# Summing two weight matrices in wider ScalarE passes, a first weight load in two halves, and new instruction sequences, in a fused attention and feed-forward kernel

## What is computed

```python
# attention part, per batch
Q, K = h @ Wq.T, h @ Wk.T                       # h: context, 4 heads
sim = einsum('bhnd,bhmd->bnm', Q, K) / (sqrt(d) * H)
threshold = top_k(sim, 153)[0][:, :, -1:]       # the 153rd largest of each row of 512
A = sigmoid(sim) * (sim >= threshold)
A = (A + A.T) * 0.5
x = x + (1 - gamma) * layernorm(x) + gamma * A
# feed-forward part
def weight_quant(w): s = 1 / clip(mean(abs(w)), 1e-5); return round(clip(w * s, -1, 1)) / s
def bitlinear(x, w): return act_quant(rmsnorm(x)) @ weight_quant(w).T
y = layernorm(x)
x = x + bitlinear(silu(bitlinear(y, w_gate)) * bitlinear(y, w_up), w_down)
```

## Time and profile before

| | |
|---|---|
| runs | 271.83, 271.90, 272.65 us; median 271.9 |
| profiled execution, own time | 272.7 us |
| its span in the trace | 269.8 us |
| busy: PE, DVE | 215.5 us (80%), 215.6 us (80%) |
| busy: ACT, POOL | 192.0 us (71%), 171.2 us (63%) |
| PE weight loads (beside the matmuls) | 105.0 us |
| DMA | 39.18 MB, mean 145 GB/s |
| mean granted PE clock | 0.911 |

### The profile page before, as it was taken

The page is one execution under the profiler, slowest core; times in us unless marked ns, Lnnn a source line. Parts: engine busy times, 40 slices in busy tenths (PEclk is TensorE's granted clock), DMA queues, the critical chain, the costliest instruction groups (busy, mean ns, idle before and its releaser), DMA issues.

```text
span 269.8 us, 3680 instructions
## 1 busy us (share of the span) xinstructions
PE 215.5 (80%) x947; PEld 105.0 (39%) x958; DVE 215.6 (80%) x379; ACT 192.0 (71%) x325; POOL 171.2 (63%) x324
## 2 busy tenths in 40 slices
PE   7744501503986896799999999999999999999985
PEld 7212101402733352343445444444544444444432
DVE  0368987998879998997999899897988787488381
ACT  2488995999999999998988967663619185241420
POOL 2045798885886868788977778886661823408330
PEclk9965755565799999999999999999999999999999
DMA  4999999979849478364104044306096115190675
GB/s 129 392 348 386 388 327 188 420 187 214 151 81 161 78 88 157 69 117 90 31 1 79 2 78 88 88 0 101 10 244 140 39 36 140 19 197 12 125 201 206
DMA packets 78998, 39.18 MB, mean 145 GB/s; under 512 B 67968, under 2 KB 70272, under 8 KB 78464
## 3 DMA queue, kind: packets, MB, share of 16 engines
q1 hardware_dynamic: 78976, 38.94, 58.6%
...
## 4 chain that ended last, share of the span: by engine, by line
PE 31%; ACT 20%; issue 15%; DVE 15%; POOLq 6%; POOL 6%; DMA 4%; DVEq 3%; ACTq 0%
PE U L394 10%; PE DN L413 10%; PE G L380 9%; ACT junk_c L491 6%; ACT S L540 5%; DVE S L741 4%; DMA S<-S 3%; ACT WdT L533 3%; DVE amh L746 2%; DVE m L607 2%; ACT sg L516 2%; ACT junk_x L505 1%; PE TR L413 1%; POOLq L911 1%; POOL X L935 1%
## 5 line engine op out<-in xcount | busy, mean ns | idle before, releaser
L380 PE MATMUL G<-WgT,xqT 128*128 128x512 bf16 x256 | 60.5, 379 | 4.7 <-ACT sg L516 4.6
L516 ACT ACTIVATE sg<-G,gsc 128x1024 f32<-128x1024 f32 x32 | 35.6, 1112 | 40.2 <-PE G L380 36.1
L394 PE MATMUL U<-WuT,xqT 128*128 128x512 bf16 x256 | 60.5, 379 | 1.7 <-DVE S L741 1.2
L491 ACT ACTIVATE junk_c<-rows,srch 128x512 int8<-128x512 f32 (+1 forms) x72 | 51.1, 716 | 5.0 <-POOL srch L904 3.3
L741 DVE TENSOR_TENSOR S<-U,sg 128x1024 f32<-128x1024 f32 x32 | 39.0, 1218 | 14.2 <-PE U L394 11.6
L1000 POOL TENSOR_SCALAR S<-S,qh 128x2048 int16<-128x2048 f32 x15 | 31.1, 2076 | 24.7 <-DVE qh L790 23.0
L413 PE MATMUL DN<-WdT,S 128*128 128x512 bf16 x198 | 45.7, 379 | 0.5
L380 PEld LDWEIGHTS G<-WgT,xqT 128*128 128x128 bf16 x256 | 24.5, 98 | 36.4 <-issue 5.5
L394 PEld LDWEIGHTS U<-WuT,xqT 128*128 128x128 bf16 x256 | 24.5, 98 | 33.7 <-DVE S L741 5.0
L746 DVE TENSOR_REDUCE amh<-S 128x1 f32<-128x2048 f32 x15 | 34.0, 2270 | 0.1
L524 ACT ACTIVATE junk_h<-S 128x2048 int8<-128x2048 f32 x16 | 30.5, 1903 | 3.7 <-DVE S L741 3.6
...
## 6 DMA issues: line engine op xcount, KB each, us to landing
...
S<-S SPq DMA_TRANSPOSE x17, 4.3
```

Of the source, the lines that this page charges most:

```text
L380: last = nc.tensor.matmul(G[:, c * 512:(c + 1) * 512], xqT[:, t, k, :], WgT[:, 4 * n:4 * n + 4, k, :], start=(k == 0), stop=(k == KD - 1))
L394: last = nc.tensor.matmul(U[:, c * 512:(c + 1) * 512], xqT[:, t, k, :], WuT[:, 4 * n:4 * n + 4, k, :], start=(k == 0), stop=(k == KD - 1))
L491: A(junk_c[:, j, :].bitcast(U8) if r == ROUNDS else junk_c[:, j, :], ROWS[a % 2][:, j, :], ACT.Sign, bias=nthr[:, j:j + 1], accum_out=cs[: ...
L516: A(sg[:, u % 2, :], G[:, :], ACT.Silu, scale=gsc[:, b % 2, t:t + 1]).then_inc(silu_done, 1)
```

## The change

Three edits:

1. Up's and down's weight sums on ACT are made in two passes of 4096 columns (`w_abs2`), not four of 2048. A pass waits for both its groups and counts as two. Their sums are added over 2 columns, not 4. (`w_round2` is defined and not called.)
2. Gate's group 0 is loaded by two DMAs of 0.5 MB, each with its own semaphore, and DVE sums it in two halves of 1024 columns (`w_abs_half`). Gate's sums are added over 5 columns.
3. All five lists are made anew.

```diff
-        wsum = sb("wsum", [P, 3, 4])
+        wsum = sb("wsum", [P, 3, 5])
...
+        s_wh = [sem(f"s_wh{h}") for h in range(2)]
...
-        n_dve = [4 * (w + 1) - n_act[w] for w in range(3)]
+        n_dve = [4 * (w + 1) + 1 - n_act[w] for w in range(3)]
+        N_SUMS = (5, 2, 2)
...
+            def w_load_half(w, h):
+
+                sp.dma_start(STAGE[w][:, h * GROUP // 2:(h + 1) * GROUP // 2].rearrange("p (c d) -> p c d", d=D),
+                             w_gate[h * 256:(h + 1) * 256, :].rearrange("(c p) d -> p c d", p=P)).then_inc(s_wh[h], 16)
...
-                nc.tensor.matmul(DN[:, 0:4], onesf[:, :], wsum[:, w, :], start=True, stop=True).then_inc(s_wtot, 1)
+                nc.tensor.matmul(DN[:, 0:N_SUMS[w]], onesf[:, :], wsum[:, w, 0:N_SUMS[w]], start=True,
+                                 stop=True).then_inc(s_wtot, 1)
...
+            def w_abs2(w, g):
+
+                for k in (g, g + 1):
+                    act.wait_ge(s_win[w][k], 16)
+                act.wait_ge(s_wabs_act, n_act[w - 1])
+                if w == 2:
+                    act.wait_ge(s_wt[0][g], 16)
+                    act.wait_ge(s_wt[0][g + 1], 16)
+                A(junk_w[w][:, g:g + 2, :], STAGE[w][:, g * GROUP:(g + 2) * GROUP].rearrange("p (c f) -> p c f", c=2),
+                  ACT.Abs, accum_out=wsum[:, w, g // 2:g // 2 + 1]).then_inc(s_wabs_act, 2)
...
-                V.tensor_reduce(wm[:, w:w + 1], DN[:, 0:4], AX.X, ALU.add)
+                V.tensor_reduce(wm[:, w:w + 1], DN[:, 0:N_SUMS[w]], AX.X, ALU.add)
...
+            def w_abs_half(w, h):
+                dve.wait_ge(s_wh[h], 16)
+                V.tensor_reduce(wsum[:, w, 4 * h:4 * h + 1], STAGE[w][:, h * GROUP // 2:(h + 1) * GROUP // 2], AX.X,
+                                ALU.add, apply_absolute_value=True).then_inc(s_wabs_dve, 1)
...
-            w_load(0, w_gate, 0); w_load(0, w_gate, 1); w_load(0, w_gate, 2); c_load(0, 1, 2); c_load(1, 2, 4)
-            w_load(0, w_gate, 3); x_load(0); x_load(1); w_load(1, w_up, 0); w_load(1, w_up, 1); w_load(1, w_up, 2)
+            w_load_half(0, 0); w_load_half(0, 1); w_load(0, w_gate, 1); x_load(0); c_load(0, 1, 2)
+            w_load(0, w_gate, 2); w_load(0, w_gate, 3); w_load(1, w_up, 0); w_load(1, w_up, 1); w_load(1, w_up, 2)
```

More of the change, by code:

```diff
@@ new lines, in _ @@
+            counts(0, 3, 0); evac_GT(1); counts(0, 3, 1); tanhs(0, 0); tanhs(0, 1); tanhs(0, 2); sims(1, 0)
+            w_abs2(1, 0); w_abs2(1, 2); tanhs(0, 3); sims(1, 1); sims(1, 2); sims(1, 3); w_round(1, 0)
+            counts(1, 0, 0); counts(1, 0, 1); w_round(1, 1); counts(1, 1, 0); counts(1, 1, 1); w_round(1, 2)
+            counts(1, 2, 0); counts(1, 2, 1); centre(0, 0); x_squares(0, 0); centre(0, 1); x_squares(0, 1)
+            centre(0, 2); x_squares(0, 2); counts(1, 3, 0); centre(0, 3); counts(1, 3, 1); tanhs(1, 0)
@@ new lines, in _ @@
+            tanhs(1, 1); evac_hT(2); tanhs(1, 2); w_abs2(2, 2); x_squares(0, 3); evac_GT(2); w_round(1, 3)
+            w_abs2(2, 0); sims(2, 0); sims(2, 1); silu(0); tanhs(1, 3); sims(2, 2); w_round(2, 0); w_round(2, 1)
+            silu(1); sims(2, 3); w_round(2, 2); w_round(2, 3); silu(2); counts(2, 0, 0); squares(0); silu(3)
+            counts(2, 0, 1); centre(1, 0); centre(1, 1); counts(2, 1, 0); silu(4); counts(2, 1, 1)
+            counts(2, 2, 0); counts(2, 2, 1); counts(2, 3, 0); silu(5); x_squares(1, 0); x_squares(1, 1)
@@ new lines, in _ @@
+            w_scale(2); x_cast(0, 2); masked(1, 0); masked(1, 1); masked(1, 2); sim_stats(2, 0, 1); x_cast(0, 3)
+            masked(1, 3); mul(0); w_quant(2, 0); sim_stats(2, 2, 3); w_quant(2, 1); mul(1); h_absmax(0)
+            h_floor(0); w_quant(2, 2); h_scale(0); w_quant(2, 3); x1(1, 0); x1(1, 1); mul(2); x_stats(2, 0, 1)
+            x_stats(2, 2, 3); mul(3); x1(1, 2); h_cast(0); x1(1, 3); x_absmax(1, 0); mul(4); h_absmax(1)
+            h_scale(1); mul(5); x_absmax(1, 1); x_absmax(1, 2); x_absmax(1, 3); x_scale(1, 0, 1, 2, 3); h_cast(1)
@@ new lines, in _ @@
+            h_absmax(2); mul(6); x_cast(1, 0, 1); rank(2, 0); rank(2, 1); rank(2, 2); rank(2, 3); note_misses(2)
+            mul(7); threshold(2); h_scale(2); x_cast(1, 2, 3); h_absmax(3); mul(8); final(0); general_path(2)
+            h_scale(3); mul(9); sim_stats(3, 0, 1); sim_stats(3, 2, 3); masked(2, 0); masked(2, 1); masked(2, 2)
+            masked(2, 3); x_stats(3, 0, 1); h_cast(2); mul(10); final(1); x1(2, 0); x_stats(3, 2, 3); h_cast(3)
+            mul(11); x1(2, 1); h_absmax(4); h_floor(1); h_scale(4); h_absmax(5); x1(2, 2); mul(12); h_scale(5)
@@ new lines, in _ @@
+            final(2); x1(2, 3); x_absmax(2, 0); x_absmax(2, 1); x_absmax(2, 2); x_absmax(2, 3)
+            x_scale(2, 0, 1, 2, 3); mul(13); final(3); h_cast(4); x_cast(2, 0, 1); mul(14); h_absmax(6); mul(15)
+            h_scale(6); h_cast(5); h_absmax(7); h_scale(7); rank(3, 0); mul(16); rank(3, 1); rank(3, 2); mul(17)
+            x_cast(2, 2, 3); final(4); h_absmax(8); h_cast(6); mul(18); h_floor(2); rank(3, 3); note_misses(3)
+            h_scale(8); h_cast(7); final(5); mul(19); threshold(3); general_path(3); masked(3, 0); masked(3, 1)
@@ L865, in _ @@
+            h_scale(13); final(10); mul(28); mul(29); final(11); h_absmax(14); h_scale(14); h_cast(13); mul(30)
+            last_absmax(0); h_cast(14); mul(31); last_absmax(1); last_scale(); last_round(0); last_round(1)
+            final(12); final(13); final(14); final(15)
         @block.gpsimd
```

173 lines of the change are left out of this document (75 added, 98 removed).

## The result

The changed kernel is slower: 275.18 us median (274.93 to 275.84, 5 runs) beside 271.9 for the kernel before (271.83 to 273.29, 5 runs), a ratio of 1.0102 (95% interval 1.0079 to 1.0125). Other chips gave the kernel before medians of 272.07 to 272.75, so each experiment is compared by its ratio to the runs of the kernel before beside it.

The account below looks back on a forecast made before the run. It took ACT and DVE to bound the front and PE the back. Loads 0, x 0 and a PE lead of 1.8 us at up(9) gave 270.9 against the profiled 272.7, or 270.1 against the median 271.9; range 267.9 to 272.6.

Parts of the forecast that it names:

- Half loads: Gate's first load in two halves on DVE: gain nothing, one more DMA costed at 0.
- x after up: Later x batches loaded behind up's groups, read at some 50 us: costed at 0.
- group 1: Rival: gate's group 1 lands late by up to 2 us and the whole front moves, 272.1; chance 0.05.
- The wide pass: ACT's sum of 4096 columns takes about 3.48, 0.3 us less for a pair; rival that it saves nothing, 270.7, chance 0.08.
- ACT between the searches: 1.9 us: One w_round fills ACT's wait before batch 1's counts, 42.6 to 44.5, counts as early as before: 1.9 us.
- ACT up to silu(0): 2.4 us: ACT's lead grows to 2.4 us, after a 0.6 wait for sims(2, 1); silu(0) ends at 79.2, not 81.6.
- DVE up to mul(8): 2.6 us: DVE, from batch 0's last x1 to mul(8): mul(8) starts at 126.8, 2.6 us earlier.
- Behind that PE is the bound: I let no gain arise or vanish: PE behind up(9) and the last similarity: the lead of 1.8 us reaches the end unchanged.
- DVE gives it back: Rival: w_quant and casts meet POOL more often, three meetings cost 2.5 and nothing is left, 271.9; chance 0.14.
- The down sum ahead of the first multiply: Rival: w_total(2) and w_scale(2), now ahead of up(0) and batch 1's masks, hold up mul(0), 272.9; chance 0.15.
- The clock at the first gates: Rival: with up(0) gone from 76 to 80, PE's clock falls to 1.2 GHz, 271.2; chance 0.03.

Follow-up runs that it names:

- b_half: The kernel before with only the first weight load split into two halves, each with its own sum on DVE: 272.07 us, ratio 1.0000.
- b_wideq: The kernel before with the wide passes only, and up's last group loaded ahead of x_load(2): 273.63 us, ratio 1.0050.
- a_narrow: The changed kernel with down's sums in four passes of 2048 again and the copy of sims(2,0) between them: 276.16 us, ratio 1.0129.
- hyb_old: The kernel before up to silu(0) and its counterparts on the other engines, the changed kernel's sequences behind: 273.86 us, ratio 1.0080.
- a_silu: The changed kernel with silu(13) moved ahead of counts(3,2,1), centre(2,1) and two x_squares on ACT: 273.62 us, ratio 1.0042.
- a_keep: The changed kernel with eight throwaway matmuls on ones added on PE between down(2,1) and gate(14): 274.37 us, ratio 1.0056.
- a_both: The changed kernel with silu(13) moved ahead of counts(3,2,1) on ACT and h_round(4) ahead of h_coef(2,2) on POOL: 273.89 us, ratio 1.0042.
- hyb_mid: The changed kernel up to about 131 us, behind that what is left in the order of the kernel before: 275.92 us, ratio 1.0127.

## Why the prediction was wrong

- **Half loads, x after up, group 1: right.** DVE's idle time ahead of the statistics grew from 2.94 to 4.00, and `b_half` is neutral. ACT's sum of group 1 starts at 11.50, where the earlier trace rows had 11.57, and the measured cost of one more load is within 0.2% of nothing. The Trainium skill ("DMA: Bandwidth & Descriptors", on the anatomy of one DMA on the gpsimd path) gives a fixed 2.0 us for each DMA. Here SP issued the loads, and nothing of such a cost shows in the time.
- **The wide pass: too cheap.** 3.60 from start to start, not 3.48: it saves 0.18 a pair, not 0.3. This term was mis-sized, by 0.12 a pair. I took the slope from counts of 512 columns, which carry a per-partition bias. The Trainium skill ("ScalarE: Activation LUTs") gives an ACTIVATE with immediate operands 186 ns and 0.833 ns per column, an estimate of 3.60 for 4096, and some 93 ns more for each pointer operand. The trace agrees (3.60, and 1.90 for 2048 columns), and my slope of 0.77 was low for that reason.
- **"ACT between the searches: 1.9 us" was right at its place and wrong behind it.** `w_round(1, 0)` ran at 42.59 to 44.50 as forecast, and then the next counts waited 1.25 for POOL.
- **"ACT up to silu(0): 2.4 us" measured 0.4.** 1.25 went there, 1.22 (forecast 0.6) in the wait for `sims(2, 1)`; the last wide pass ended at 77.8, not at 76.3. The pass over 4096 columns makes this wait itself: it swallowed the gap in which the first copy stood. `b_wideq` has the same wait, and with passes of 2048 in `a_narrow` it is gone.
- **"DVE up to mul(8): 2.6 us" measured 0.4** (129.05 for 129.43). The last `x1` started at 59.17, not at 57.5, with waits of 1.77 and 0.72 for POOL's `add_a` on the way, and `x_cast(0, 0)` at 65.28, not at 64.0. What follows waits once more, 1.28 for `w_total(2)` (80.29). `mul(0)` was 1.8 late, not 0.15. The runs say more: with `mul(0)` anywhere from 83.01 to 85.36, PE is through the last similarity within 0.7 us (the table). I had carried a lead from one engine's list to the next as if the idle times between would stay; the chain passes over all engines, and each takes a part of it.
- **"Behind that PE is the bound: I let no gain arise or vanish" is the step that failed.** It was right that PE has no idle time there in the kernel before. But the order that keeps it busy is one of the things that the change replaces, so it had to be read again for the new lists. I named `up(18)` and `gate(24)` as tight; `up(18)` waits 0.25 (182.16) and `gate(24)` not at all. The place was `gate(14)`, a gap of over 1 us behind 130, which the prediction does list among its signs of being wrong, and ACT's new list between `silu(12)` and `silu(13)` would have shown it: four counts, two centres and two squares, 154.65 - 148.39 = 6.3 us with the wait for POOL, and 1.1 for `silu(13)` itself, where PE has `gate(13)` and `down(2, *)`, 1.73 + 3.45 = 5.2 us, to cover it. Of the 5.3 between forecast and result in PE's times, 3.2 are this step and 2.1 the front (a lead of 1.8 that came out as 0.3 late). `hyb_old`, with the old front and the new sequences, has the wait too (1.93), and `a_silu`, with one `silu` moved, has not.
- **The rivals.** DVE gives it back: this is what happened in the front (forecast 271.9 by itself). The down sum ahead of the first multiply: the last wide pass ended 1.5 later than my count, short of the 2.6 from which I let it decide, and `w_scale(2)` did wait 1.28 for it ahead of the masks; it took its part of the front's lead and is not what made the kernel slower. The clock at the first gates: not in the changed kernel's own profile, but in those of `a_keep`, `a_both` and `hyb_mid`, which have its front; its 0.03 was too low. None had a wait behind 132, so the range's upper end, 272.6, was too low by 2.6.

What stays open: how often the clock falls behind 154. What a fall costs is 1.69 by the profile, 1.7 by the table (3.2 against 1.5), and 1.6 by the lower group of `a_keep`. Of the changed kernel's five executions four have spans of 273.3 to 273.7 and one has 271.7, so it may be most of them; only one was traced. Nor is it known which order of the stretch from 131 to 180 would hold without a wait behind the new front.
